# Projections of an attention block: fp32 products replaced by three float32r products of operands split on chip

## The reference, cut to what matters

```python
q = (x @ Wq.T).reshape(B, S, H, D)      # k and v alike; B, S = 4, 1024; H, D = 32, 16
q = rope(q, cos, sin); k = rope(k, cos, sin)
#   rope: [x1 * cos - x2 * sin, x1 * sin + x2 * cos] over the two halves of D
scores = q @ k.T * D**-0.5 + bias;  causal mask
m = max(max(scores), offset);  p = exp(scores - m)
out = (p @ v) / (sum(p) + exp(offset - m));  out = out @ Wo.T
x = layernorm(x + out)
x = layernorm(x + quant(x) @ quant(Wff).T + bff)
```

## Time and profile before

| what | value |
|---|---|
| median of 3 runs | 1701.8 us (1701.53 to 1702.06) |
| the profiled execution | 1702.25 us, its span 1700.4 us |
| TensorE busy | 1619.2 us, 95% of the span |
| VectorE, ScalarE, GpSimd busy | 1266.4, 1089.8, 230.3 us |
| mean granted TensorE clock | 0.983 of full speed |
| stage 1 | first matmul at 9.43 us, last `take_up` at 363.46 us |

### The profile page before, as it was taken

One profiled execution on the slowest core, in us unless ns is written; L12 is line 12 of the kernel. 1 busy time (PEld: TensorE's weight loads), 2 busy tenths in 40 slices (PEclk: granted clock), 3 DMA queues, 4 the chain that ended last, 5 costly groups with the idle time before them and its releaser, 6 DMA issues. The chain is left out here.

```text
span 1700.4 us, 27915 instructions
## 1 busy us (share of the span) xinstructions
PE 1619.2 (95%) x9168; PEld 753.2 (44%) x9168; DVE 1266.4 (74%) x3812; ACT 1089.8 (64%) x1576; POOL 230.3 (14%) x125
## 2 busy tenths in 40 slices
PE   7999999989999999999999999999999999899984
PEld 3444444434444444444444444444444444344431
DVE  2454666668788887888888878888888786179995
ACT  2333333347878788878877887878787888534442
POOL 4333323220000000000000000000000000034342
PEclk9999999999999999999999999999999999999995
DMA  5447463535533543444433543363345402012221
GB/s 221 148 149 230 141 179 124 161 124 84 105 51 52 115 75 51 88 70 83 84 56 64 91 86 51 59 118 64 51 89 81 71 14 88 13 62 81 94 75 50
DMA packets 124501, 156.97 MB, mean 92 GB/s; under 512 B 14915, under 2 KB 80515, under 8 KB 124102
## 3 DMA queue, kind: packets, MB, share of 16 engines
q1 hardware_dynamic: 124358, 155.19, 39.1%
HBM read 103.90 MB, written 50.46 MB: 91 GB/s over the span
## 5 line engine op out<-in xcount | busy, mean ns | idle before, releaser
L930 ACT ACTIVATE probs<-ps 128x1024 f32<-128x1024 f32 (+3 forms) x768 | 592.3, 810 | 178.9 <-PE ps L694 120.0
L1179 DVE CUSTOM_DVE_ANT_0 junk<-ps,bias_q 128x384 bf16<-128x384 f32 (+2 forms) x1024 | 502.0, 502 | 136.7 <-PE ps L667 125.3
L688 PE MATMUL ps<-q_stack,k_stack 99*128 99x512 bf16 (+3 forms) x1536 | 489.6, 328 | 12.8 <-ACT ps L945 4.4
L667 PE MATMUL ps<-k_stack,q_stack 96*128 96x384 bf16 (+3 forms) x1536 | 491.7, 333 | 10.5 <-DVE mx L1179 3.8
L1172 DVE TENSOR_REDUCE mx<-ps 128x1 f32<-128x128 f32 (+3 forms) x768 | 365.3, 485 | 42.4 <-PE ps L667 35.1
L760 PE MATMUL ps<-attn 128*128 128x512 f32 x768 | 346.9, 595 | 11.1 <-DMA attn<-hT 9.4
L694 PE MATMUL ps<-bias_r,ident_r 128*128 128x384 f32 (+2 forms) x1280 | 352.5, 363 | 0.0
L709 PE MATMUL ps<-probs,v_sb 128*32 128x512 f32 (+3 forms) x3072 | 328.2, 499 | 0.1
L667 PEld LDWEIGHTS ps<-k_stack,q_stack 96*128 96x128 bf16 x1536 | 142.3, 97 | 368.0 <-DVE mx L1172 136.7
L694 PEld LDWEIGHTS ps<-bias_r,ident_r 128*128 128x128 f32 x1280 | 222.4, 193 | 37.0 <-issue 0.2
L760 PEld LDWEIGHTS ps<-attn 128*128 128x128 f32 x768 | 142.8, 191 | 172.9 <-issue 160.1
(11 more groups left out here) (103 smaller groups left out, 1011.4 us busy)
## 6 DMA issues: line engine op xcount, KB each, us to landing
q_stack<-q_parts SPq DMA_DIRECT2D x192, 128.0 KB, 4.3
v_dram<-v_sb SPq DMA_DIRECT2D x32, 512.0 KB, 2.6
v_sb<-v_dram SPq DMA_DIRECT2D x32, 512.0 KB, 9.6
k_stack<-k_parts SPq DMA_DIRECT2D x32, 384.0 KB, 7.3
q_parts<-q_stack SPq DMA_DIRECT2D x84, 128.0 KB, 2.0
k_parts<-k_stack SPq DMA_DIRECT2D x84, 128.0 KB, 2.9
attn<-hT SPq DMA_DIRECT2D x8, 1024.0 KB, 7.0
k_stack<-k_parts SPq DMA_DIRECT2D x32, 256.0 KB, 8.0
```

The lines of the kernel that those rows point to most:

```text
L667: pe.matmul(ps_ring[:, use.bank, 0:c1 - c0], q_stack[0:STACK, b, hl, I * P:(I + 1) * P], k_stack[0:STACK, b, hl, c0:c1], start=True, stop= ...
L688: mm = pe.matmul(ps_s[:, u % 2, hh, 0:w], k_stack[0:ROWS, b, hl, J * P:(J + 1) * P], q_stack[0:ROWS, b, hl, i0:i0 + w], start=not in_bank, ...
L930: act.activation(probs[:, (u // 2) % 3, 2 * pr:2 * pr + 2, 0:w], ps_s[:, pr, :, 0:w], ACT.Exp).then_inc(exp_done, 1)
L1179: ins = dve.tensor_tensor_reduce(out=junk[:, use.bank, 0:c1 - lo], in0=ps_ring[:, use.bank, lo - c0:c1 - c0], in1=bias_q[:, hl, BAND - t0 ...
```

## The change

1. **Products.** The weights and each input chunk are split on chip into a float32r high part (ScalarE copy, `weight_hi`, `operand_hi`) and the difference (VectorE for the weights, GpSimd `operand_lo` for the chunks). Each fp32 matmul becomes three float32r matmuls: high x high, high x low, low x high. The split operands lie in a buffer of `attn`'s size laid over it.
2. **Storage.** There is now one split chunk at a time. The last three tiles of a chunk run with the slices `kt` outermost, and each slice signals `hT_left`, so that ScalarE can write the next chunk's slice. ScalarE's copies stand at pair 2 of a chunk (slice 0 after `take_up`, 1 after `first_part`, 2 after `second_part`) and ahead of pair 3's `take_up` (slice 3). GpSimd's four subtractions stand after pair 2's sine.
3. **Rotary turn.** `raw` moves to the small buffers, and there is no `by_sin`: GpSimd multiplies `raw` by the sine in place, and waits for VectorE's `by_cos` of the same pair to have read it. `third_part` moves from after `rot` to right after the next pair's `by_cos`.
4. **Tables.** The rope tables are reloaded in pieces of 512 columns per chunk, four transfers a chunk.
5. **Start.** Wq and the first chunk come in slices; Wk is loaded into Wq's input buffer once Wq has been split, and all twelve weight copies stand ahead of the first `take_up` in ScalarE's list.
6. **First maxima** are spread over the 120 places of pairs 12 to 31 (`beside`); on VectorE three places stand ahead of `by_cos` and three between `third_part` and `rot`.
7. The loop over groups in GpSimd's `take_bias` is written out, and `bias_r` is two tensors.

```diff
-                pool.wait_ge(raw_ready, FIRST + b * 8 + pair + 1)
-                pool.wait_ge(rot_ready, FIRST + b * 16 + 2 * (pair - 1))
-                pool.tensor_tensor(by_sin[q % 2], raw[:, q % 2, :, :],
-                                   rope_cs[:, 1, q % 2, c:c + 1, :].broadcast_to([P, 2, CH]),
+                pool.wait_ge(raw_read_dve, FIRST + b * 8 + pair + 1)
+                pool.wait_ge(rope_loaded[q % 2], 32 * (2 * b + c + 1))
+                pool.tensor_tensor(raw[q % 2], raw[q % 2], rope_sin[q % 2].unsqueeze(1).broadcast_to([P, 2, CH]),
                                    ALU.mult).then_inc(sin_ready, 1)
+            def operand_lo(chunk, kt):
+                pool.wait_ge(hT_hi, NK * chunk + kt + 1)
+                pool.tensor_tensor(hT_r[:, 1, kt, :], hT_in[kt], hT_r[:, 0, kt, :].bitcast(FP32),
+                                   ALU.subtract).then_inc(hT_lo, 1)
...
+            def beside(pair, place):
+                slot = (pair - BESIDE_0) * PLACES + place
+                slots = (PAIRS - BESIDE_0) * PLACES
+                found = [m for m in range(2 * NM) if m * slots // (2 * NM) == slot] if slot >= 0 else []
...
+            def products(chunk, i, kt):
+                tile = chunk * 12 + i
+                w = 2 if i % 3 == 2 else i // 6
+                for first, second in ((0, 0), (0, 1), (1, 0)):
+                    if w < 2:
+                        m = i % 3 * 2 + i // 3 % 2
+                        lhsT = w_r[:, first, w, kt, m * P:(m + 1) * P]
+                        rhs = hT_r[:, second, kt, :]
...
+                    mm = pe.matmul(ps[:, RING + tile % PBANKS, :], lhsT, rhs, start=(kt == 0 and first + second == 0),
+                                   stop=(kt == NK - 1 and first == 1))
...
+            sp.wait_ge(w_lo[0], NK)
+            sp.dma_start(w_in[2], wkT.rearrange("(k p) n -> p k n", p=P)).then_inc(w_loaded[NK + 1], 16)
...
+            for kt in range(NK):
+                weight_hi(0, kt)
+                operand_hi(0, kt)
+            for w in (2, 1):
+                for kt in range(NK):
+                    weight_hi(w, kt)
             for done in range(PAIRS):
+                more = done // 4 + 1 < 2 * B
+                if done % 4 == 3 and more:
+                    operand_hi(done // 4 + 1, 3)
                 take_up(done)
+                if done % 4 == 2 and more:
+                    operand_hi(done // 4 + 1, 0)
                 if done < PAIRS - 1:
                     first_part(done)
+                    if done % 4 == 2 and more:
+                        operand_hi(done // 4 + 1, 1)
                     second_part(done)
+                if done % 4 == 2 and more:
+                    operand_hi(done // 4 + 1, 2)
...
                 dve.tensor_tensor(by_cos, raw[q % 2], rope_cos[q % 2].unsqueeze(1).broadcast_to([P, 2, CH]),
                                   ALU.mult).then_inc(raw_read_dve, 1)
+                if done:
+                    third_part(done - 1)
+                for place in range(3, PLACES):
+                    maximum(place)
```

More of the change, by code:

```diff
@@ L119 @@
 PAIRS = B * 8
+BESIDE_0 = 12
+PLACES = 6
 FIRST_ORDER = [(0, k) for k in range(NM)] + [(1, k) for k in range(4)] + [(0, "M")] + [(1, k) for k in range(4, NM)]
@@ L262, in build @@
         ext_k_dram = dram("ext_k_dram", [H, EXT], FP32)
+        with nc.sbuf_tensor("split", [P, 2, NK * 4, DM], FP32R) as split:
+            w_r = split[:, :, 0:12, :].rearrange("p s (w k) n -> p s w k n", w=3)
+            hT_r = split[:, :, 12:16, :]
         attn = sb("attn", [P, TOK // P, DM])
@@ L1100, in _ @@
                     turn_by_sine(b, pair)
+                    chunk = 2 * b + pair // 4 + 1
+                    if pair % 4 == 2 and chunk < 2 * B:
+                        for kt in range(NK):
+                            operand_lo(chunk, kt)
                     if pair == 0 and b >= 2:
@@ L1115, in _ @@
             pool.wait_ge(ones_set, 5)
-            with pool.Fori(0, G - 1) as g:
-                take_bias(g + 1, (g + 1) % 2)
+            for g in range(1, G):
+                take_bias(g, g % 2)
             pool.wait_ge(ring_read, Use(G - 1, 1, NM - 1, LAST_GROUP).before + 1)
@@ L1244, in turn_pair, with maximum @@
                 buf = part_turn(done)[0]
-                def maximum(i):
-                    if b >= 2:
-                        k = 6 * pair + i
-                        if (b, k) == (3, 4):
-                            split_shifts(0, Use.first(0, "M"))
-                        max_unit(0, k, b - 2, Use.first(b - 2, k))
-                for i in range(3):
-                    maximum(i)
+                last = done == PAIRS - 1
+                def maximum(place):
+                    m = beside(done, place)
+                    if m is None:
+                        return
+                    n, k = m // NM, m % NM
+                    if m == NM + 4:
+                        split_shifts(0, Use.first(0, "M"))
+                    max_unit(0, k, n, Use.first(n, k))
+                    if k == NM - 1:
+                        shifts(0, n, n, Use.first(n, k))
@@ L1256, in turn_pair @@
+                for place in range(3):
+                    maximum(place)
                 dve.wait_ge(raw_ready, FIRST + done + 1)
-                dve.tensor_tensor(by_cos, raw[:, q % 2, :, :],
-                                  rope_cs[:, 0, q % 2, c:c + 1, :].broadcast_to([P, 2, CH]),
+                dve.wait_ge(rope_loaded[q % 2], 32 * (2 * b + c + 1))
+                dve.tensor_tensor(by_cos, raw[q % 2], rope_cos[q % 2].unsqueeze(1).broadcast_to([P, 2, CH]),
                                   ALU.mult).then_inc(raw_read_dve, 1)
-                maximum(3)
+                if done:
+                    third_part(done - 1)
@@ L1266, in turn_pair @@
                                   ALU.add).then_inc(rot_ready, 1)
-                last = done == PAIRS - 1
-                if last:
-                    maximum(4)
-                    maximum(5)
-                    shifts(0, 1, 1, Use.first(1, NM - 1))
-                if pair:
-                    third_part(done - 1)
                 if last:
```

207 lines of the change are left out of this document (128 added, 79 removed).

## The result

The changed kernel takes **1718.54 us** (median of 4 runs, 1718.07 to 1718.83) against 1701.66 us before (4 runs on the same chip, 1700.17 to 1702.06): ratio 1.0101, 95% interval 1.0083 to 1.0118. It is 1% slower, and the interval lies clear of no change. 1716 was predicted. The two profiled executions have spans of 1716.1 and 1700.4 us, so there are 15.7 us to account for.

The account below looks back on a forecast made before the run. It took the serial ring of ScalarE, VectorE and GpSimd as the new bound: 31 x 10.49 + 21.4 + 2.4 + 2.4 = 351.4 against 343.9, +7.5; start +7.6, seam -1.2: +13.9, so 1716 us, range 1702 to 1732.

Parts of the forecast that it names:

- What bounds the kernel: Stage 1: TensorE bound before, can give back 0.9 us a pair; the 69 us it saves become idle time.
- Products: Stage 1 on TensorE: a float32r product of 512 columns takes 0.228 us, 8.2 us a pair instead of 10.36.
- the rival of exposed loads: Stage 1: weight loads not hidden, 0.42 us a product, TensorE the bound again, 1865 us; chance 0.03.
- The ring: Stage 1: the serial chain of ScalarE, VectorE and GpSimd from take-up to take-up becomes the bound, 10.49 us a pair.
- ring shorter: Rival, stage 1: sine and `third_part` run side by side, 9.5 us a pair, 29 us less, 1687 us; chance 0.09.
- Chunk changes: Stage 1, 7 times: slice copies, a delayed `rot` and a late `by_cos` add 3.05 us each, 21.4 in all.
- Maxima, bias split and stacks: Stage 1: colliding maxima add 2.4 us, the bias split behind pair 16 adds 2.4; no term for the stacks' load.
- The clock: Rival, stage 1: TensorE's idle gaps bring its clock to 1.2 GHz, 1762 us if in most pairs; chance 0.10.
- the rival's second half: Stage 1: the clock falls in most pairs; at a quarter of (16.4 - 10.5) a pair, 46 us, 1762.
- The start: Ahead of stage 1's ring: splitting Wq, then fetching and splitting Wk, puts the first take-up at 27.1, +7.6 us.
- The seam: Between stage 1's last take-up and the start of stage 2: 1 to 2 us shorter, taken as -1.2 us.
- From there on nothing differs: From stage 2 on: the same operations are issued, so stage 2 takes as long as before.

Follow-up runs that it names:

- e3: The changed kernel with only the high x high product, the two mixed products left out; 1714.6 us (one run).
- e1: The changed kernel with VectorE's `third_part` moved back behind `rot`; 1701.4 us, ratio 0.9999 to the kernel before.
- e4: The changed kernel with Wk's copies and subtractions moved after the first take-up, into pair 0; 1718.5 us, ratio 1.0102 to the kernel before.
- a2: The kernel before with 42 more instructions on VectorE ahead of stage 2, which only count a semaphore up; 1714.2 us, ratio 1.0073.
- a1: The changed kernel with 7 more instructions on VectorE ahead of stage 2, which only count a semaphore up; 1722.0 us, ratio 1.0123 to the kernel before.
- b1: The changed kernel with its first maxima in pairs 16 to 31 instead of 12 to 31; 1722.6 us, ratio 1.0123 to the kernel before.
- e2: e1 with each take-up moved ahead of the second part of the pair before; 1674.8 us, ratio 0.9853 to the kernel before.
- e5: e2 with the first maxima over pairs 14 to 31 instead of 12 to 31; 1682.0 us, ratio 0.9886 to the kernel before.
- s1: The kernel before with the sine waiting for `by_cos` and `third_part` between `by_cos` and `rot`, fp32 products kept; 1710.3 us (one run).
- p3: The kernel before with GpSimd's `take_bias` loop over groups written out; 1700.1 us (one run).
- p1: The kernel before with 14 unused semaphores allocated ahead of the others; 1702.6 us (one run).
- p2: The kernel before with an unused buffer of 512 columns; 1702.9 us (one run).

## Why the prediction was right, and where it wasn't

- **What bounds the kernel: right.** What TensorE saved became idle time. e3 shows it: two thirds of the products less change the common step by nothing. The saving is 44 us of busy time in the whole span (1619.2 to 1574.9), not 69. An estimate of the rest: 1152 products at 0.231 instead of 0.228 make 3.5 us, and the granted clock of 0.94 in the mean from 24 to 376 us some 21.
- **Products: right.** 0.231 us against 0.228. (The lower bound, 0.213, makes 7.7 us a pair, not 8.0; nothing rests on it.) The weight load (0.20 us in the mean) is hidden, so the rival of exposed loads is out. The Trainium skill, "TensorE: Matmul & The Clock Gate", in its part on row and column tiling, has loads overlap only when the row group differs. The trace disagrees with that sentence, here as in the earlier trace rows.
- **The ring: right**, 10.49 predicted and 10.49 measured. By its own step the sine would end 2.21 after `third_part`; it ended 40.09 - 37.85 = 2.24 after. e1 shows that the 0.91 us are the meeting of GpSimd's multiplication and VectorE's `third_part`, and that was the decisive point of the rival "ring shorter". The Trainium skill, "SBUF — State Buffer", in its section on the two separate sides of SBUF, has VectorE and GpSimd share a port pair that the one which starts first holds for its whole instruction, also where VectorE's operation only has two inputs in SBUF. The trace agrees: the sine ends 2.24 after `third_part`, nearly the 2.40 that it takes alone.
- **Chunk changes: right** in the sum (3.00 against 3.05) and in the parts: ScalarE's two copies 57.43 - 56.39 = 1.04 (1.2), `rot` 1.67 - 0.69 = 0.98 (1.1), the late `by_cos` and its collision 0.98 (0.75), which is what is left of the 3.00.
- **Maxima, bias split and stacks:** 350.65 - 31 x 10.49 - 7 x 3.00 = 4.5 us against 4.8. The sum is right by luck, for two of its four parts were not foreseen: 2.0 at pair 11 to 12, where TensorE waits 6.8 us for the stacks' load, and -0.95 in the first step, which takes 9.54 because no `third_part` meets the sine in it. The bias split behind pair 16 is 2.2 (2.4 predicted). The collisions of the maxima, 2.4 in the prediction, can then be only the 1.1 that are left.
- **The clock: right.** It does fall. Near the first chunk's change TensorE stood idle from 42.4 to 46.0, and its granted clock fell to 0.50, until 49.1:

```profile
45.70:49.00 3.30, 3.01 (x7) 2.43 (x8) 2.36 (x2) 1.35 (x3) 1.73 (x1) 0.50 0.39 159
```

  The Trainium skill, "TensorE: Matmul & The Clock Gate", in its part on the clock gate, has idle gaps bring the half clock back; the trace agrees. The mean in stage 1 is 0.93 to 0.94, and the rival's second half (a quarter of (16.4 - 10.5) in each pair) doesn't follow, since TensorE's idle time takes it up: the step in which it fell, 44.93 to 57.43, takes 12.50, and one of the same kind without a fall, 181.89 to 194.40, takes 12.51. e3 at 0.65 is the stronger proof.
- **The start: the mechanism was right, the term was mis-sized**, +7.6 for +5.35. The table load, which was put behind the fills at 10.6, ran at 4.03, beside them: 1.28 us. With this, Wk was sent for at 17.1 instead of 18.6. The other 0.7 are in its way from there to the first take-up, 7.8 us where 8.5 were taken: it had landed 5.7 after it was sent for, near the lower bound, and the four copies took 2.1. e4 shows that moving the copies into pair 0 doesn't help.
- **The seam: right** in the sum, -1.20; its parts were not taken apart.
- **"From there on nothing differs": this step failed.** Stage 2 took 6.02 us more. It issues the same operations, but each of its steps is 0.18 us longer (29 of them: 5.1 us), as VectorE's list is 42 instructions longer ahead of it and its steps stand elsewhere modulo 64. a2 shows it in the kernel before. The remaining 0.9 us are in the first step: some 0.2 are the same late operation, and the rest goes with the granted clock (0.89 instead of 0.91 over that step, and longer steps at a lower clock in the other kernels too). What follows the last mark came out 1.2 shorter for the clock alone.

In sum 13.9 - 2.25 - 0.75 + 4.8 = 15.7. The forecast came within 2.5 us in part by luck: the start's 2.3 too many and the 4.8 missing in stages 2 and 3 (+6.0 - 1.2) partly cancel. The ring and the chunk changes, 31 x 10.49 and 7 x 3.0, were right for their own reasons.

## What to carry to other kernels

Before an engine is relieved, work out the next ring link by link: here TensorE had 0.9 us a pair to give before the ring of ScalarE, VectorE and GpSimd bound the stage, and an operation moved one place (`third_part`, to a slot beside GpSimd's multiplication) took that back; moving it back and taking the next pair up before the last part of the one before made the same cheaper products worth 1.5%. An input that waits for a store and a reload, as the first maxima do for the stacks, sets the earliest pair, and a shorter ring runs into it. When two profiles of the same loop differ by a fixed small time each step, look for the one row that is late, and for its place in its engine's list. Ahead of that, compare the granted clock over both stretches: it can differ between two runs of one kernel.

## What was not expected of the hardware

- An operation of VectorE that stands at a multiple of 64 in the engine's list can start 0.27 to 0.36 us late: in the changed kernel (9.70 to 10.04 us into the step), in a1 (8.20 to 8.54), in b1 (11.82 to 12.09) and in a2 (9.70 to 10.06). Not each one is late, and what the engine does there wasn't found. The profile's DMA part lists two packets of the instruction queue q14 a step, which come at 17.3 and 28.6 us into the step in the changed kernel and at 1.8 and 22.3 in the kernel before; none falls on the late operation, so no cause is read from them.
- 42 instructions that only count a semaphore up held VectorE for about 4 us, some 0.1 us each.
- At a granted clock of 0.65 in the mean (e3), stage 1 was no slower.
- The time behind the last mark of stage 2 goes in three levels, by one fall of the granted clock some 60 us behind the mark. Where it stays at 1.00 there, the time is 291.4 to 292.1 us (after, e2, e3, e5, s1, p3); where it is 0.50 for 3.4 us, 293.0 to 293.6 (before, a2, e4, p1, p2); where it is 0.50 for 6.8 us, 294.2 to 294.8 (e1, a1, b1). The kernel before has both kinds of run: some near 1700.1 us at a mean clock of 0.986 and some near 1702.2 at 0.983. So two single runs should not be compared to a microsecond without it.
